# Second pass over the edges in a graph network: half of the scaled columns made by the scalar engine, and the clearing of the sums put ahead of the wait for messages

## The reference, cut to what is touched

```python
z = jnp.concatenate([atom_features[dst], atom_features[src], edge_features], axis=1)
signal = jax.nn.softplus(_batchnorm(z @ W_core.T + b_core, gamma_core, beta_core))
gate = jax.nn.sigmoid(_batchnorm(z @ W_filter.T + b_filter, gamma_filter, beta_filter))
message = gate * signal
nbr_sumed = jax.ops.segment_sum(message, dst, num_segments=atom_features.shape[0])
return atom_features + nbr_sumed
```

## Time and profile before

| what | value |
|---|---|
| median of 3 runs | 14130.92 us |
| lowest and highest | 14119.66 us and 14131.49 us |
| the profiled execution's own time | 14130.73 us |
| span of its trace, first to last instruction | 14128.6 us |
| mean granted TensorE clock over the span | 0.663 |
| DVE busy | 6544.2 us (46%) |
| ACT busy | 1956.4 us (14%) |
| POOL busy | 8845.0 us (63%) |

### The profile page before, as it was taken

The page is one execution under the profiler, slowest core; times in us unless marked ns, Lnnn a source line. Parts: engine busy times, 40 slices in busy tenths (PEclk is TensorE's granted clock), DMA queues, the critical chain, the costliest instruction groups (busy, mean ns, idle before and its releaser), DMA issues.

```text
span 14128.6 us, 163232 instructions
## 1 busy us (share of the span) xinstructions
PE 6607.3 (47%) x40537; PEld 5667.4 (40%) x40538; DVE 6544.2 (46%) x13266; ACT 1956.4 (14%) x3267; POOL 8845.0 (63%) x8158
## 2 busy tenths in 40 slices
PE   4777777774655555688600000085333334333333
PEld 3777777774555555677600000074111112111112
DVE  4444444444566666799700000198443434444344
ACT  0111111110222222466400000000000001000000
POOL 0888888886577777300177777501777774777773
PEclk7666666665777777899855555597555556555556
DMA  4333333333344444333222222232111111111111
GB/s 92 18 18 18 18 18 18 18 18 50 108 125 126 126 126 126 113 98 99 64 51 54 54 55 54 54 97 73 39 39 39 39 39 35 39 39 39 39 39 28
DMA packets 851570, 827.51 MB, mean 59 GB/s; under 512 B 630205, under 2 KB 636579, under 8 KB 848948
## 3 DMA queue, kind: packets, MB, share of 16 engines
q0 software_dynamic: 450064, 387.16, 18.6%
q1 hardware_dynamic: 401470, 439.92, 9.9%
HBM read 571.32 MB, written 255.06 MB: 58 GB/s over the span
## 4 chain that ended last, share of the span: by engine, by line
POOL 52%; issue 22%; PE 11%; DMA 8%; DVE 5%; SPq 2%; DVEq 1%; POOLq 0%; ACT 0%; ACTq 0%
POOL tab L728 21%; POOL aux L702 10%; POOL lane_tab L685 10%; DMA lane_tab<-rows,idx 8%; POOL buf_b L702 6%; POOL acc_w L702 5%; PE ps L1077 3%; PE ps L1188 1%; PE ps L1124 1%; PE ps L1110 1%; PE ps L967 1%; DVE buf_b L1631 1%; PE ps L957 1%; POOL t_first_tab L713 1%; PE ps L1073 1%
## 5 line engine op out<-in xcount | busy, mean ns | idle before, releaser
L728 POOL DMA_INDIRECT tab<-gcn_tab,idx x3136 | 2982.7, 951 | 1808.3 <-issue 1806.7
L685 POOL DMA_INDIRECT lane_tab<-rows,idx x1664 | 2595.9, 1560 | 797.2 <-issue 796.0
L1089 PE MATMUL ps<-ident_b,zero_b 128*128 128x512 bf16 x1664 | 778.8, 623 | 2912.5 <-issue 1606.8
L1710 DVE TENSOR_REDUCE buf_d<-ps 128x512 f32<-128x1536 f32 x416 | 731.2, 1758 | 2299.4 <-PE ps L1093 2299.4
L702 POOL DMA_INDIRECT aux<-att_tab,idx x1568 | 1485.6, 947 | 477.8 <-issue 477.8
L1089 PEld LDWEIGHTS ps<-ident_b,zero_b 128*128 128x128 bf16 x1664 | 182.7, 128 | 3277.3 <-issue 1831.6
L702 POOL DMA_INDIRECT buf_b<-src_tab,idx x832 | 843.2, 1014 | 457.6 <-issue 253.5
L991 PE MATMUL ps<-ident,srcg 128*128 128x128 f32 x3328 | 706.7, 398 | 690.4 <-DVE srcg L1339 690.3
L702 POOL DMA_INDIRECT acc_w<-src_tab,idx x832 | 815.1, 980 | 253.6 <-issue 249.9
L991 PEld LDWEIGHTS ps<-ident,srcg 128*128 128x128 f32 x3328 | 654.0, 301 | 737.2 <-DVE srcg L1339 737.2
L1167 PE MATMUL ps<-ident,acc_w 128*128 128x128 f32 x13 | 3.0, 423 | 1953.6 <-ACT idx L816 1953.6
(11 more groups left out here) (296 smaller groups left out, 14373.1 us busy)
## 6 DMA issues: line engine op xcount, KB each, us to landing
y_stash<-buf_c SPq DMA_DIRECT2D x208, 512.0 KB
tab<-y_stash SPq DMA_DIRECT2D x208, 512.0 KB, 3.3
aux<-in_edge_attr_dram SPq DMA_DIRECT2D x1696, 32.0 KB
h_stash<-aux SPq DMA_DIRECT2D x196, 264.0 KB, 2.1
tab<-gcn_tab,idx POOLq DMA_INDIRECT x3136
buf_c<-h_stash SPq DMA_DIRECT2D x156, 264.0 KB, 2.7
lane_tab<-rows,idx POOLq DMA_INDIRECT x1664, 3.2
aux<-att_tab,idx POOLq DMA_INDIRECT x1568
```

The costliest lines, as they stand in the source:

```text
L685: pool.indirect_dma_start(lane_tab[k][:, :], bass.IndirectOffsetOnAxis(ap=idx[:, b, u:u + 1], axis=0), rows[:, b, u, 0:D1], None, compute_ ...
L728: pool.indirect_dma_start(g_rows[k][:, u, :], None, table[:, :], bass.IndirectOffsetOnAxis(ap=idx[:, k % RING, u:u + 1], axis=0)).then_inc ...
L1089: pe.matmul(ps[:, 4 * (q % 2) + c, :].rearrange("p (k f) -> p k f", f=P), zero_b[:, :], bc(ident_b[:, :].unsqueeze(1), [P, 4, P]), start=T ...
L1710: dve.tensor_reduce(g_sum[b], parts(4 * b), AX.X, ALU.add).then_inc(s.split_joined, 1)
```

## The change

Scaling is split by columns. DVE scales columns 0 to 511 as before. Columns 512 to 1023 are scaled by ACT in two instructions that read PSUM: an Abs into `log_buf` and a Relu into `z_buf`, each with `bn_col` as scale and bias. The softplus on DVE stays as it is, since max(relu(z), 0) is relu(z). ACT's Abs of columns 0 to 511 reads `z_buf` as before. The counts on `l1b_act` go from three a group to five, and `lb_turn` now also waits for the Relu of two groups ago.

`add_group` is written out in `lb_sums`, in another order: the wait for the previous addition, the clearing, `load8`, then the waits for one-hot and messages, then the eight matmuls.

```diff
+            act.wait_ge(s.bn_ready, 1)
+
             def lb_logs(t, k, age):
                 if age < 2 * ITER:
                     a = log_buf[:, k % 2, :]
-                    act.wait_ge(s.l1b_normed, t + 1)
+                    y = ps_flat[:, (k % 2) * 1024 + 512:(k % 2) * 1024 + 1024]
+                    act.wait_ge(s.l1b_turned, t + 1)
                     if age >= 2:
                         act.wait_ge(s.l1b_softplus, t - 1)
-                    act.activation(a, z_buf[:, k, :], ACT.Abs).then_inc(s.l1b_act, 1)
-                    act.wait_ge(s.l1b_act, t * 3 + 1)
+                    act.activation(a[:, 512:1024], y, ACT.Abs, bias=bn_col[:, 1:2], scale=bn_col[:, 0:1]).then_inc(s.l1b_act, 1)
+                    if age >= 4:
+                        act.wait_ge(s.l1b_back, t - 3)
+                    act.activation(z_buf[:, k, 512:1024], y, ACT.Relu, bias=bn_col[:, 1:2], scale=bn_col[:, 0:1]).then_inc(s.l1b_act, 1)
+                    act.wait_ge(s.l1b_normed, t + 1)
+                    act.activation(a[:, 0:512], z_buf[:, k, 0:512], ACT.Abs).then_inc(s.l1b_act, 1)
+                    act.wait_ge(s.l1b_act, t * 5 + 3)
                     act.activation(a, a, ACT.Exp, scale=-1.0).then_inc(s.l1b_act, 1)
-                    act.wait_ge(s.l1b_act, t * 3 + 2)
+                    act.wait_ge(s.l1b_act, t * 5 + 4)
                     act.activation(a, a, ACT.Ln, bias=1.0).then_inc(s.l1b_act, 1)
...
                 if age >= 2:
                     pe.wait_ge(s.l1b_normed, g - 1)
+                    pe.wait_ge(s.l1b_act, g * 5 - 8)
...
             def lb_sums(g, q):
+                pe.wait_ge(s.l1b_added, g + 1)
+                for c in range(2):
+                    pe.matmul(ps[:, 6 + c, :].rearrange("p (k f) -> p k f", f=P)[:, :, 0:D1], zero_b[:, :],
+                              bc(ident_b[:, 0:D1].unsqueeze(1), [P, 4, D1]), start=True, stop=False, skip_group_check=True)
+                rel = load8(mybir.EngineType.PE, rel_s, g, (G - 1) * P)
                 pe.wait_ge(s.l1b_hot, g + 1)
                 pe.wait_ge(s.l1b_messages, g + 1)
-                pe.wait_ge(s.l1b_added, g + 1)
-                add_group(lb_hot[q], lb_rows[q % 2], g, 6, D1).then_inc(s.l1b_sums, 1)
+                for u in range(G):
+                    last = pe.matmul(ps_flat[:, bass.ds(rel[u] + 6 * 512, D1)], lb_hot[q][:, u, :], lb_rows[q % 2][:, u, 0:D1],
+                                     start=False, stop=True, skip_group_check=True)
+                last.then_inc(s.l1b_sums, 1)
...
-                    dve.tensor_scalar(z_buf[:, k, :], ps_flat[:, (k % 2) * 1024:(k % 2) * 1024 + 1024], scale, shift, ALU.mult, ALU.add).then_inc(s.l1b_normed, 1)
+                    dve.tensor_scalar(z_buf[:, k, 0:512], ps_flat[:, (k % 2) * 1024:(k % 2) * 1024 + 512], scale, shift, ALU.mult, ALU.add).then_inc(s.l1b_normed, 1)
...
-                    dve.wait_ge(s.l1b_act, t * 3)
+                    dve.wait_ge(s.l1b_act, t * 5)
```

More of the change, by code:

```diff
@@ L1067, in _ @@
             pe.wait_ge(s.bn_ready, 1)
[L1069 to L1079, removed]
             def aggregate(left_ready, conv, free, done):
```

## The result

| kernel | median | lowest to highest | runs |
|---|---|---|---|
| before | 14131.37 us | 14118.31 to 14138.69 us | 16 |
| changed | 14154.05 us | 14143.74 to 14167.65 us | 16 |

The ratio is 1.0016, with a 95% interval of 1.0009 to 1.0023: the change costs 23 us (13 to 33), 0.16%. The forecast was 14130 us, no change. The time lies in the range (14086 to 14158) and under the 0.2% bound, but it moved, and not the way that the sum said. The profiled execution of the changed kernel took 14154.35 us.

The account below looks back on a forecast made before the run. The message loop, 5.22 us a step, was taken to bound the kernel; afterwards the log loop, 4.70 + 1.14 + 1.68 + 1.84 + 1.07 = 10.43 for two steps, 5.215 each, saves 1 us: 14130 us, range 14086 to 14158.

Parts of the forecast that it names:

- the sum: Log loop after the change, gate to softplus through back to gate: 10.43 us for two steps, 5.215 a step, saving 1 us.
- The bound: DVE, busy 276.71 of 300 us, isn't full; it waits for the gate, and a loop of 5.22 us sets the pace.
- The message loop: Gate, messages, clearing, first product, back transposes, next gate: closes in one step, 5.22 us before, 4.33 after the change.
- the log loop: Gate, ACT's logs, softplus, addition, products, back transposes, gate: closes in two steps, 10.10 us before, 10.43 after.
- The signs: Expected in the changed profile: uneven gate starts, DVE idle some 0.5 us before softplus, products 0.88 us after the clearing.
- Two bounds beside the loop: Per-step limits of engines by themselves after the change: ACT 4.70 us, DVE 4.35 us.
- The four operands: Scale and shift from `bn_col` on ACT's two PSUM activations: 0.09 us each, 0.37 us in all.
- The long steps: 21 steps of 5.9 to 6.0 us instead of 5.22, with slower back transposes; carried over unchanged, 5 us in the range.
- Rival (b): PE's register load doesn't run ahead of the messages wait: x us to products instead of 0.10, deciding from 0.38; chance 0.10.
- (a): ACT's operands are hidden: 5.03 us a step, 14091 us; chance 0.24 in full or with a faster load, halfway 0.07.
- (c): ACT's three pieces each 0.1 us dearer than rows of other shapes say: +31 us, 14162 us; chance 0.06.
- (d): DVE was the bound, the halved scaling worth 0.53 us each step: 4.69 us a step, 14020 us; chance 0.03.

## Why the prediction was right or wrong

**The bound.** Right. DVE's 92% was no bound: with the split alone its work fell and 130 us came on top. The wait of the messages for the gate was the sign of it.

**The message loop.** Right: with clearing and load ahead, it no longer counts. With the order alone, where the same terms gave 4.75 a step for the log loop and 4.80 for DVE by itself, 4.765 was measured. Of the two the log loop decides; DVE by itself is 4.73.

**The log loop after the change.** Right, to 0.02 us in two steps: 10.43 forecast, 10.45 measured, with 4.65 for gate to softplus instead of 4.70 and 1.73 for addition to products instead of 1.68. The signs came too, if not all in their size: the wait ahead of the softplus is 0.87 us on average instead of 0.5, and products follow the clearing after 0.98 instead of 0.88. Two bounds beside the loop were put too high, without harm: ACT passes a group in 4.54 us (the short step) and not 4.70, and DVE's 4.35 had a wait for Ln in its 1.27 from one-hot to softplus.

**The four operands.** Right: taken at 0.37 by one row of another shape, and measured at 0.36. The figure of some 93 ns for each pointer operand, which the Trainium skill gives in "ScalarE: Activation LUTs", section "What ACT_TABLE_LOAD costs", is borne out by this with two operands on one instruction. The advice of its section "Rules for kernel authors" to use VectorE for relu came true here, but by the loop in which ACT stands (the split alone costs 130 us), not by the price of a column.

**The long steps.** Wrong, and this is the step of the prediction that failed: "Both loops contain the back transposes, so I carry these over", and, in the range, that the delay "may partly be made up". The rows I stood on showed the cause, a granted clock of 0.97 with transposes of 1.84 us instead of 1.04. I took the falls as something that comes to the kernel from outside and stays as it is. They depend on what PE does: extra PE work in a step of unchanged length took the clock from 0.93, and from 0.97, to 0.99, in three kernels. The changed kernel has the same PE instructions in the same two steps, but its idle time is placed otherwise (1.2 us in a row in every other step beside 0.53 to 0.59 in each, instead of 0.58 and 0.50 in each), and the clock falls twice at each of 19 places, instead of once at each of 21. 15 us became about 45 us, and the ends of the pass took 7 us more. Added to a sum that is right otherwise, that gives +36.5 us in the pass, and 23 us (13 to 33) in the time.

**Rival (b)** was true in kind, at 0.25 us instead of 0.10, and below the point from which it decides. **(a)** was wrong: the operands aren't hidden. **(c)** was wrong: the pieces were 0.77, 0.78 and 0.64, where I had 0.78, 0.78 and 0.62. **(d)** was wrong. None of my rivals had the clock in it, and the mechanism on the slower side that I did name was not the one that made it slower.

**What stays open.** What makes the second fall of a pair. More PE work in a step of the same length keeps the clock up, in the changed kernel at either of two places and in the kernel before. But the amount of work in a given time doesn't order all kernels: the one without operands has 3930 PE instructions in its 600 us and a clock of 0.95, the kernel before 3850 and 0.97, the one with the load first 3955 and 0.99. Nor does the sum of PE's idle time in two steps: it is some 1.8 us both without the operands (0.95) and with the second clearing (0.99), 2.2 in the kernel before (0.97) and 2.3 in the changed one (0.93). Where the idle time lies is a candidate, and no experiment moved it alone. The piece of 1.1 to 1.2 us in every other step doesn't do it by itself: the changed kernel has it with the second clearing and with the load first too, and there no pairs and two pairs are left.

## What to carry to other kernels

Before counting what an edit frees, write down every loop that closes through the engines, with the number of steps in which it closes: here one of one step was 0.17 us ahead of one of two, and while one half of the change shortened both, the other half lengthened the second again, which was then the one that decided. What an engine that is 92% busy waits for tells more than its busy share, and work moved to an engine with more idle time can be dearer there when that engine stands in the loop. Where the granted clock in a stretch is below 1.00, its losses are a term of the sum that changes with PE's pattern: ask what the edit does to PE's idle time, and put a range on it.

## What the hardware showed

- Matmuls that compute nothing made two kernels faster: a second clearing, 0.39 us of PE work in idle time, took the changed kernel from 23 us above before to its level (11 us below, interval 23 below to 3 above), and the kernel before down by 22 us (6 to 35). The clock in the pass went from 0.93, and 0.97, to 0.99.
- The same PE instructions in the same 10.45 us lost 15 us to the clock over 21 places in one arrangement and about 45 us over 19 in the other.
- From the end of what PE waits for to the first product behind a register load, 0.99 us in the kernel before and 1.04 in the changed one; with the load done ahead, 0.25 us; to the clearing, whose wait stands on the matmul, 0.05 to 0.10 us.
- Vector instructions overlap by some 0.08 us, so a busy share of 100% can hide a wait: with the order alone DVE shows 600.00 of 600 us busy and still waits for Ln, at 4.765 us a step where it can do 4.73.
